# Weights of the gate and up projections placed 64 bytes further on in SBUF, in a cross-attention and FP4 feed-forward kernel

## The chip, the cores and the metric

The kernel runs on one core of a Trainium2 chip. The metric is the device time of one execution in microseconds (us), as the median of several runs. Times inside an execution are read from one profiled run.

## The reference, cut to what matters

The input `x` has 2 x 2048 rows of 512 numbers, and the context has 2 x 77 rows. All is float32. The second layer, on which the change bears, rounds its inputs and weights to a 4-bit grid in blocks of 16:

```python
x = x + xattn(layernorm(x), ctx, ctx)        # 16 heads of 32, causal, 77 keys
def ffn(x):                                  # x 512 wide, hidden 1408 wide
    gate = fp4_linear(x, w_gate)
    y = fp4_linear(x, w_up)
    return fp4_linear(silu(gate) * y, w_down)
x = x + ffn(layernorm(x))
```

## The kernel before, in words

**Tiles and stages.** The 4096 rows are 32 tiles of 128 (`T`). `attention` handles tile after tile: the query projection into `q_ps`, scores, probabilities, values, and the output projection into `w_ps`. Beside it, it rounds the feed-forward weights piece by piece. `feed_forward` then takes the 32 tiles again. In its iteration `a`, TensorE (PE) does `gate(a, c)` and `up(a, c)` for four chunks `c` of 352 hidden columns (`GU_N`), and then `down(a - 2)`, 33 matmuls with 512 columns into `d_ps`. Between chunk 0 and chunk 1 stands one small transposition (L1410). The order on every engine is written out by hand, and tiles 4 to 29 run in a hardware loop.

**Products in three parts.** A product of two float32 matrices is made of a high and a low half of each operand: `split_matmuls` (L177 to L179) issues three matmuls for each of the four slices `d` of 128 input columns, that is 12 for one `gate` or `up` and 12 for one projection:

```python
pe.matmul(out, lh, rh, start=(i == 0), stop=False)      # L177
pe.matmul(out, lh, rl, start=False, stop=False)         # L178
last = pe.matmul(out, ll, rh, start=False, stop=...)    # L179
```

The first operand is stationary: it is loaded into the array before the matmul (LDWEIGHTS, PEld in the profile). The second is moving: it is read from SBUF while the matmul runs. For `gate` and `up` the stationary operand is a slice of `xnh` or `xnl` (`hqh` and `hql` for tile 1 alone, by `halves_of`), and the moving one is 352 columns of `wguh` or `wgul`, 1408 bytes in each partition. These two hold the gate weights in their first 1408 columns and the up weights in the other 1408. For `down` it is `hqh` or `hql` and 512 columns of `wd`, save for the last two tiles, whose halves lie in the space of `wguh` and `wgul` and whose sums go to `u_ps`.

**Places in SBUF.** `sbuf_tensor` gives each tensor the next free place, in the order in which the program asks, rounded up to 32 bytes in a partition. `attention` and `feed_forward` each use the space that lies behind `Shared` and `FfnInput`, one after the other. `wguh` and `wgul` lie over the tensors of `Setup`, which are dead by the time the weights are written there.

From this follow the places below, as the remainder of a tensor's first byte by 256. A slice `d` of `wguh` is 11264 bytes on (44 x 256), the up half is 5632 bytes on (22 x 256), and chunk `c` is `c` x 1408 bytes on (5.5 x 256), so chunks 0 and 2 have the tensor's own remainder and chunks 1 and 3 lie 128 beside it. The slices of all other operands here are whole multiples of 256 apart.

| tensor | role | before | changed |
|---|---|---|---|
| `wguh`, `wgul`, chunks 0 and 2 | moving, 352 | 128 | 192 |
| `wguh`, `wgul`, chunks 1 and 3 | moving, 352 | 0 | 64 |
| `xnh`, `xnl` | stationary | 0 | 0 |
| `hqh`, `hql` | stationary | 192 | 64 |
| `wd` | moving, 512 | 192 | 64 |
| `wqh`, `wql` | moving, 512 | 224 | 96 |
| `woh`, `wol`; `ath`, `atl` | moving, 512; stationary | 224 | 96 |
| `ident` | moving of the transposes | 128 | 192 |
| `att`; `probs`; `q` | stationary of the transposes | 224; 96; 32 | 96; 224; 160 |
| `xin`, `xn` | rows of x | 0 | 192 |

Of the kernel before, what the change touches and what calls it, by code (L numbers as in the profile page):

```python
# [9 lines left out]
F32R = mybir.dt.float32r  # L10
# [6 lines left out]
P = 128  # L17
B, SEQ, E = 2, 2048, 512
# [3 lines left out]
EC = E // P  # L22
# [41 lines left out]
RING = 5  # L64
# [25 lines left out]
class Part:  # L90


    def __init__(self, lo=None, hi=None):
        self.cols = slice(lo, hi)
        self.blocks = slice(lo and lo // BLK, hi and hi // BLK)
# [111 lines left out]
class Shared:  # L207


    def __init__(self, ctx, nc):  # L210
        sb = lambda name, shape, dt=F32: ctx.enter_context(nc.sbuf_tensor(name, shape, dt))
        self.setup = Setup(nc)
        self.wguh, self.wgul = sb("wguh", [P, EC, 2 * FF], F32R), sb("wgul", [P, EC, 2 * FF], F32R)
        self.ident = sb("ident", [P, P])

        self.half_neg, self.eps = sb("half_neg", [P, 1]), sb("eps", [P, 1])
        self.minus_one, self.over_qmax = sb("minus_one", [P, 1]), sb("over_qmax", [P, 1])

        self.xin = sb("xin", [P, RING, E])
        self.xn = sb("xn", [P, E])  # L220
        self.xnh, self.xnl = sb("xnh", [P, EC, P], F32R), sb("xnl", [P, EC, P], F32R)
        self.w_q = sb("w_q", [P, E])
        self.quant = Quant(ctx, nc, "quant", E)

        self.xn_ps = ctx.enter_context(nc.psum_tensor("xn_ps", [P, 512], F32))
        self.x1_stored, self.wd_stored = ctx.enter_context(nc.semaphore("x1_stored")), ctx.enter_context(nc.semaphore("wd_stored"))
# [1561 lines left out]
```

## Time and profile before

| | |
|---|---|
| median of 3 runs | 1170.78 us (1170.64 to 1171.21) |
| the profiled execution | 1172.72 us, its span 1170.9 us |
| TensorE (PE) busy | 1151.4 us, 98% of the span |
| weight loads (PEld) busy | 1042.8 us, 89% |
| VectorE (DVE) busy | 970.1 us, 83% |
| ScalarE (ACT) busy | 482.4 us, 41% |
| GpSimd (POOL) busy | 180.0 us, 15% |
| granted TensorE clock | full through the span |

The span is the time from the first to the last instruction in the profile; the execution's own time holds what lies around it. Matmuls overlap in the profile: a matmul's duration includes the time until its last result is out, and the next one starts before that. What one matmul costs in a dense run is therefore the distance between two starts. The timeline gives starts to 0.01 us, so over 23 distances in a row the mean is known to about 0.5 ns.

### The profile page before, as it was taken

How to read it: one execution, taken by the hardware profiler on the slowest of the kernel's cores; microseconds unless marked ns; L12 is line 12 of the kernel's file. 1: busy time of each engine (PE TensorE's matmuls, PEld its weight loads, DVE VectorE, ACT ScalarE, POOL GpSimd, SP SyncE). 2: the span in 40 equal slices, each digit the busy share in tenths (PEclk: the TensorE clock that was granted, in tenths of full speed). 3: DMA queues.
4: the chain of work that ended last, by engine and by line, in shares of the span. 5: the costliest groups of instructions: out<-in, count | busy, mean ns of one | idle time of the engine just before them, and what ended most of it. 6: DMA issues, size and time to landing. Idle time of an engine off the chain costs nothing.

```text
span 1170.9 us, 21792 instructions
## 1 busy us (share of the span) xinstructions
PE 1151.4 (98%) x6916; PEld 1042.8 (89%) x6916; DVE 970.1 (83%) x1609; ACT 482.4 (41%) x1201; POOL 180.0 (15%) x305
## 2 busy tenths in 40 slices
PE   7899999999999989999999999999999999999998
PEld 6688888888888889999999999999999999999997
DVE  6778888888888877898888888888888888888865
ACT  3556656565666642333322333333333223323321
POOL 2433333333333310100000000000000000000000
PEclk9999999999999999999999999999999999999999
DMA  7133332333445327563454335444533554453352
GB/s 241 35 101 105 92 105 91 104 100 101 141 132 156 120 87 226 118 115 70 94 98 90 88 82 102 81 90 95 96 79 88 99 87 88 87 106 71 84 84 45
DMA packets 139473, 119.26 MB, mean 102 GB/s; under 512 B 91637, under 2 KB 102981, under 8 KB 139180
## 3 DMA queue, kind: packets, MB, share of 16 engines
q1 hardware_dynamic: 139436, 118.83, 43.2%
q8 instruction: 16, 0.26, 0.1%
q14 instruction: 21, 0.17, 0.1%
HBM read 74.47 MB, written 24.94 MB: 85 GB/s over the span
## 4 chain that ended last, share of the span: by engine, by line
PE 91%; DVE 4%; ACT 2%; issue 1%; DMA 1%; POOL 0%; SPq 0%; DVEq 0%; ACTq 0%; POOLq 0%
PE g_ps L177 7%; PE u_ps L177 7%; PE g_ps L178 7%; PE u_ps L178 7%; PE u_ps L179 7%; PE g_ps L179 7%; PE d_ps L1443 6%; PE d_ps L1444 6%; PE d_ps L1442 6%; PE o_ps L792 6%; PE s_ps L730 3%; PE s_ps L772 2%; PE w_ps L177 2%; PE q_ps L178 2%; PE q_ps L179 2%; PE q_ps L177 2%
## 5 line engine op out<-in xcount | busy, mean ns | idle before, releaser
L177 PE MATMUL g_ps<-wguh,xnh 128*128 128x352 f32 x496 | 162.4, 327 | 0.5 <-issue 0.5
L177 PE MATMUL u_ps<-wguh,xnh 128*128 128x352 f32 x496 | 159.9, 322 | 0.4 <-DVE hid L1583 0.4
L178 PE MATMUL u_ps<-wgul,xnh 128*128 128x352 f32 x496 | 159.8, 322 | 0.0
L178 PE MATMUL g_ps<-wgul,xnh 128*128 128x352 f32 x496 | 159.8, 322 | 0.0
L179 PE MATMUL u_ps<-wguh,xnl 128*128 128x352 f32 x496 | 159.6, 322 | 0.0
L179 PE MATMUL g_ps<-wguh,xnl 128*128 128x352 f32 x496 | 159.5, 322 | 0.0
L905 ACT ACTIVATE probs<-s_ps,nsmax 128x77 f32<-128x77 f32 x512 | 114.1, 374 | 88.1 <-DVE nsmax L997 88.1
L1583 DVE TENSOR_TENSOR hid<-u_ps,silu 128x352 f32<-128x352 f32 x128 | 66.9, 523 | 77.7 <-PE u_ps L179 75.5
L1444 PE MATMUL d_ps<-wd,hql 128*128 128x512 f32 x330 | 128.9, 391 | 0.0
L1443 PE MATMUL d_ps<-wd,hqh 128*128 128x512 f32 x330 | 128.9, 391 | 0.0
L1442 PE MATMUL d_ps<-wd,hqh 128*128 128x512 f32 x330 | 128.4, 389 | 0.0
L1485 ACT ACTIVATE silu<-g_ps 128x352 f32<-128x352 f32 x128 | 58.6, 461 | 133.5 <-PE g_ps L179 133.5
L276 POOL TENSOR_TENSOR nmean<-f_mv,minus_one 128x1 f32<-128x1 f32 x32 | 6.1, 192 | 637.7 <-DVE f_mv L271 637.7
L148 ACT ACTIVATE quant_magic<-quant_z 128x512 bf16<-128x512 f32 x65 | 41.1, 633 | 132.1 <-DVE quant_z L142 79.5
L177 PEld LDWEIGHTS g_ps<-wguh,xnh 128*128 128x128 f32 x496 | 93.1, 188 | 2.6 <-issue 0.9
L178 PEld LDWEIGHTS g_ps<-wgul,xnh 128*128 128x128 f32 x496 | 93.3, 188 | 1.1
L177 PEld LDWEIGHTS u_ps<-wguh,xnh 128*128 128x128 f32 x496 | 93.1, 188 | 0.8 <-DVE hid L1583 0.7
L179 PEld LDWEIGHTS u_ps<-wguh,xnl 128*128 128x128 f32 x496 | 93.4, 188 | 0.0
L179 PEld LDWEIGHTS g_ps<-wguh,xnl 128*128 128x128 f32 x496 | 93.4, 188 | 0.0
L178 PEld LDWEIGHTS u_ps<-wgul,xnh 128*128 128x128 f32 x496 | 93.2, 188 | 0.0
L792 PEld LDWEIGHTS o_ps<-vbd,probsT 128*128 128x128 f32 (+1 forms) x640 | 73.9, 191 | 5.1 <-issue 5.0
L792 PE MATMUL o_ps<-vbd,probsT 128*128 128x66 f32 (+2 forms) x640 | 78.2, 277 | 0.0
(177 smaller groups left out, 2524.6 us busy)
## 6 DMA issues: line engine op xcount, KB each, us to landing
scale_wide<-st_dram SPq DMA_DIRECT2D x248, 88.0 KB, 3.4
xin<-in_x_dram SPq DMA_DIRECT2D x32, 256.0 KB, 2.7
x_dram<-x SPq DMA_DIRECT2D x32, 256.0 KB, 2.2
xin<-x_dram SPq DMA_DIRECT2D x32, 256.0 KB, 2.7
out_dram<-y SPq DMA_DIRECT2D x32, 256.0 KB, 2.0
scale_wide<-st_dram SPq DMA_DIRECT2D x248, 32.0 KB, 1.8
w_wide<-ws_dram SPq DMA_DIRECT2D x30, 256.0 KB
wd_dram<-wd_out SPq DMA_DIRECT2D x11, 512.0 KB, 3.5
```

The source lines that it names most:

```text
L148: s.activation(self.magic[:, part.cols], self.z[:, part.cols], ACT.Copy, scale=ULP_SHIFT).then_inc(self.shifted_ready, 1)
L177: pe.matmul(out, lh, rh, start=(i == 0), stop=False)
L178: pe.matmul(out, lh, rl, start=False, stop=False)
L179: last = pe.matmul(out, ll, rh, start=False, stop=(i == n - 1))
L730: last = pe.transpose(s_ps[0:rows, i // 4, (i % 4) * P:(i % 4 + 1) * P], probs[:, at:at + rows], ident[:])
L792: last = pe.matmul(o_ps[:, half, h0 * VW:(h1 + 1) * VW], probsT[0:rows, i, :], vbd[0:rows, b, half, c, 0:(h1 - h0 + 1) * VW], start=(c == ...
L905: last = act.activation(probs[:, h * CTX:(h + 1) * CTX], s_ps[:, bank, i * CTX:(i + 1) * CTX], ACT.Exp, bias=nsmax[:, at:at + 1], scale=1.0)
L1442: pe.matmul(total, high[:, c, :], wd[:, 0, c, :], start=(c == 0), stop=False)
L1443: pe.matmul(total, high[:, c, :], wd[:, 1, c, :], start=False, stop=False)
L1444: summed = pe.matmul(total, low[:, c, :], wd[:, 0, c, :], start=False, stop=(c == FC - 1))
L1485: act.activation(silu[:, c % 2, :], g_ps[:, c % 2, 0:GU_N], ACT.Silu).then_inc(silu_ready, 1)
L1583: dve.tensor_tensor(hid[:, c * GU_N:(c + 1) * GU_N], u_ps[:, c % 2, 0:GU_N], silu[:, c % 2, :], ALU.mult).then_inc(hid_ready, 1)
```

## The change

Sixteen float32 columns (64 bytes in a partition) that nothing uses are asked for ahead of `Setup`, and so ahead of `wguh` and `wgul`. Another 64 unused bytes stand ahead of `xnh`, and the four one-column constants move from ahead of `xin` to behind `xnl`. Together these leave `xnh` and `xnl` at the byte where they were. All that is asked for behind them lies 128 bytes further on, except the constants themselves. No instruction is added, removed or moved on any engine; only addresses differ.

```diff
     def __init__(self, ctx, nc):
         sb = lambda name, shape, dt=F32: ctx.enter_context(nc.sbuf_tensor(name, shape, dt))
+        sb("ahead_of_wguh", [P, 16])
         self.setup = Setup(nc)
         self.wguh, self.wgul = sb("wguh", [P, EC, 2 * FF], F32R), sb("wgul", [P, EC, 2 * FF], F32R)
         self.ident = sb("ident", [P, P])
 
+        self.xin = sb("xin", [P, RING, E])
+        self.xn = sb("xn", [P, E])
+        sb("ahead_of_xnh", [P, 16])
+        self.xnh, self.xnl = sb("xnh", [P, EC, P], F32R), sb("xnl", [P, EC, P], F32R)
         self.half_neg, self.eps = sb("half_neg", [P, 1]), sb("eps", [P, 1])
         self.minus_one, self.over_qmax = sb("minus_one", [P, 1]), sb("over_qmax", [P, 1])
-
-        self.xin = sb("xin", [P, RING, E])
-        self.xn = sb("xn", [P, E])
-        self.xnh, self.xnl = sb("xnh", [P, EC, P], F32R), sb("xnl", [P, EC, P], F32R)
         self.w_q = sb("w_q", [P, E])
```

## Rows read from the trace of the kernel before

**Rows 1.** The page: engines' busy time, and the chain that ended last, by engine.
```profile
PE 1151.4 (98%) x6916; PEld 1042.8 (89%) x6916; DVE 970.1 (83%) x1609; ACT 482.4 (41%) x1201; POOL 180.0 (15%) x305
...
PE 91%; DVE 4%; ACT 2%; issue 1%; DMA 1%; POOL 0%; SPq 0%; DVEq 0%; ACTq 0%; POOLq 0%
```

**Rows 2.** PE's waits: who waited for whom, us in total, times, longest.
```profile
PE tp L651 <- DMA w_nat<-in_L_xattn_Wk_dram: 4.8, 1, 4.8
PE w_ps L721 <- DVE att L1010: 2.6, 1, 2.6
PE tp L651 <- DMA w_nat<-in_L_xattn_Wq_dram: 1.8, 1, 1.8
```

**Rows 3.** Timeline of PE, tile 15: start us, duration us, the instruction.
```profile
760.61 0.32 PE L177 MATMUL g_ps<-wguh,xnh 128*128 128x352 f32 x1
...
764.25 0.32 PE L179 MATMUL u_ps<-wguh,xnl 128*128 128x352 f32 x1
764.41 0.27 PE L1410 MATMUL hq_ps<-ident,scale_cols 128*120 128x128 f32 x1
```

**Rows 4.** The same: chunk 1's second matmul, the first of chunks 2 and 3.
```profile
764.68 0.33 PE L178 MATMUL g_ps<-wgul,xnh 128*128 128x352 f32 x1
...
768.39 0.32 PE L177 MATMUL g_ps<-wguh,xnh 128*128 128x352 f32 x1
...
772.19 0.33 PE L177 MATMUL g_ps<-wguh,xnh 128*128 128x352 f32 x1
```

**Rows 5.** The same: the first matmul of down, and of tile 16.
```profile
776.03 0.39 PE L1442 MATMUL d_ps<-wd,hqh 128*128 128x512 f32 x1
...
783.55 0.32 PE L177 MATMUL g_ps<-wguh,xnh 128*128 128x352 f32 x1
```

**Rows 6.** Timeline of PE, tile 1: bounds of chunks 0, 1, 2 and 3.
```profile
445.01 0.32 PE L178 MATMUL g_ps<-wgul,hqh 128*128 128x352 f32 x1
...
448.53 0.32 PE L179 MATMUL u_ps<-wguh,hql 128*128 128x352 f32 x1
...
449.94 0.32 PE L178 MATMUL g_ps<-wgul,hqh 128*128 128x352 f32 x1
...
453.63 0.32 PE L177 MATMUL g_ps<-wguh,hqh 128*128 128x352 f32 x1
...
457.46 0.32 PE L177 MATMUL g_ps<-wguh,hqh 128*128 128x352 f32 x1
...
461.14 0.32 PE L179 MATMUL u_ps<-wguh,hql 128*128 128x352 f32 x1
```

**Rows 7.** Timeline of PE, attention: the query projection, and the transposes behind it.
```profile
295.36 0.40 PE L178 MATMUL q_ps<-wql,xnh 128*128 128x512 f32 x1
...
297.69 0.39 PE L179 MATMUL q_ps<-wqh,xnl 128*128 128x512 f32 x1
297.92 0.60 PE L721 MATMUL w_ps<-ident,att 128*128 128x128 f32 x4
298.36 1.25 PE L730 MATMUL s_ps<-ident,probs 128*128 128x128 f32 x10
299.45 0.60 PE L698 MATMUL q_ps<-ident,q 128*128 128x128 f32 x4
```

**Rows 8.** Timeline of PE: the output projection, second and twelfth matmul, one iteration.
```profile
300.57 0.40 PE L178 MATMUL w_ps<-wol,ath 128*128 128x512 f32 x1
...
302.88 0.39 PE L179 MATMUL w_ps<-woh,atl 128*128 128x512 f32 x1
```

**Rows 9.** The same, the iteration that was entered after a wait.
```profile
95.89 0.40 PE L178 MATMUL w_ps<-wol,ath 128*128 128x512 f32 x1
...
98.17 0.39 PE L179 MATMUL w_ps<-woh,atl 128*128 128x512 f32 x1
```

**Rows 10.** Timeline of PE, tile 2, chunk 0: second and last matmul.
```profile
461.62 0.32 PE L178 MATMUL g_ps<-wgul,xnh 128*128 128x352 f32 x1
...
465.28 0.33 PE L179 MATMUL u_ps<-wguh,xnl 128*128 128x352 f32 x1
```

## The prediction, made before the changed kernel was run

> **What bounds the kernel now.** I read the page first, then PE's waits, then PE's timeline. The page shows PE busy for 98% of the span and on 91% of the chain that ended last [rows 1]. The reader should then see in the list of waits that PE's longest are single events: 4.8 us for the first weights, 2.6 us and 1.8 us elsewhere [rows 2]. None of them comes back with each tile, so in both stages the next matmul starts as soon as PE can take it. The time is the sum of distances between PE's starts, and a change that moves no instruction can only act by making those distances longer or shorter, or by slowing another engine so far that PE waits.
>
> The distances are the third thing to read, in tile 15, one of 26 that run in the same loop. Chunk 0 has 24 matmuls, 23 distances from 760.61 to 764.25: 3.64 / 23 = **158.3 ns** [rows 3]. Chunk 1 from its second matmul to the start of chunk 2 takes 3.71 us for 23 distances, **161.3 ns**; chunk 2 takes 3.80 us for 24, **158.3 ns** [rows 4]; chunk 3 takes 3.84 us for 24, **160.0 ns** [rows 4, 5]. These four groups do the same work, with the same shapes, at the full clock. What differs between even and odd chunks is the remainder of the moving operand, 128 against 0, while the stationary operand has 0 in both. So the place matters, by about 2 to 3 ns in 160.
>
> **Which relation matters.** The distances depend either on the moving operand's own remainder, or on its difference from the stationary one. Two places speak for the difference. The output projection and the down projection both have a difference of 0, at remainders 224 and 192. The output projection runs at 2.31 / 10 = 231 ns [rows 8], and in the iteration entered after a wait at 2.28 / 10 = 228 ns [rows 9]; the down projection runs at 7.52 / 33 = 227.9 ns [rows 5]. The query projection, equally wide but with a difference of 224, runs at 2.33 / 10 = 233 ns [rows 7]. Equal differences lie closer together than unequal ones, though by little.
>
> **Gate and up, the term of the sum.** After the change the stationary operand stays at 0 and the moving one is at 192 in chunks 0 and 2 and at 64 in chunks 1 and 3. The trace of before already holds these differences once. Tile 1 takes its stationary operand from `hqh` and `hql`, at 192, so its differences are 128 - 192, that is 192 by 256, in the even chunks, and 0 - 192, that is 64, in the odd ones. Its distances are 3.52 / 22 = 160.0 ns in chunk 0, 3.69 / 23 = 160.4 in chunk 1 (whose first few are still settling), 3.83 / 24 = 159.6 in chunk 2 and 3.68 / 23 = 160.0 in chunk 3 [rows 6]. I take **160.0 ns for all four**. Per tile that is now 24 x (158.3 + 161.3 + 158.3 + 160.0) = 15.31 us, and then 96 x 160.0 = 15.36 us: +0.05 us. Over the 30 tiles 2 to 31, **+1.5 us**. The bounds of this term are the other rhythms that 352-column matmuls show. From below, 158.3 ns in all chunks is 15.20 us, -0.11 us a tile, -3.3 us in all. From above stands tile 2's chunk 0, with 3.66 / 22 = 166.4 ns at the usual addresses [rows 10]: a chunk that runs so costs 24 x 6.4 = 0.15 us a tile, +4.6 us over 30 tiles. I take the value of tile 1, because it alone has the differences in question.
>
> **The query projection.** Its difference goes from 224 to 96, and no row has 96. It has 12 matmuls in each of 32 tiles, 384. If the new place gave the 227 to 228 ns of the down projection, it would save 5 to 6 ns each, -2.3 us; the mirror of it, +2.3 us, is my upper bound, since nothing wider than 233 ns stands in the trace at this width. I take 0: 96 and 224 are both an odd multiple of 32, and 233 ns is the only row with such a difference.
>
> **Output and down projections.** All their operands move by 128 together, so the difference stays 0 and I take 0. What may alter is the entry. The output projection settles only after some matmuls, and how it is entered decides between 231 and 228 ns: 0.03 us a tile, -1.0 us at most over 32. The down projection's 7.52 us could fall to 33 x 227 = 7.49, another -0.9 us. An entry worse than the present ones has no row, and I allow the same +1 us. The last two tiles' down matmuls change their difference from 64 to 128, but there are only 66 of them.
>
> **Transposes and everything else.** The `ident` and `xn` places change too. The transposes behind the query projection come at 0.44 / 4 = 110 ns and 1.09 / 10 = 109 ns [rows 7], with three different remainders among their stationary operands and no difference between them: 0. DMA, VectorE, ScalarE and GpSimd work on moved tensors, all still at multiples of 32 bytes. PE waits for none of them in the loops [rows 2], and VectorE has 17% of the span free [rows 1], so a small change there is hidden. If that cover were gone, it would show as a new PE wait in every tile.
>
> **A rule of the Trainium skill against the rows.** What the rows show is that the same matmul takes 158.3 or 161.3 ns by its place [rows 3, 4]. The Trainium skill, "TensorE: Matmul & The Clock Gate", section "Step-by-step: what each phase is for", states that PE has two independent SBUF read ports, and that "Loading the next tile's weights doesn't steal SBUF read bandwidth from the running matmul". By that rule the relation between the two addresses could not matter, and the change would cost 0. This trace does not agree as far as the 2 to 3 ns go, and only for matmuls that read one column per clock; the transposes do agree. The rule keeps a chance below, as a rival.
>
> **The sum.** +1.5 + 0 + 0 = +1.5 us. The profiled execution has 1172.72 us, and its span is 1170.9; the median of the runs is 1170.78, 1.9 lower than the profiled one. The term is the same in both, so the median should go to 1170.78 + 1.5 = **1172.3 us**. About 0.2%, 2.3 us, is what a measurement of this kernel can tell from no change, so this counts as within 0.2%.
>
> **The rivals.**
> - *Faster: a shorter rhythm.* The short rhythm of 158.3 ns appears at difference 128, and tile 1 may be too short a sample to show that the loop falls into it also at 64 and 192. For it: chunk 1 and chunk 3 have the same differences by 256 and still run at 161.3 and 160.0, so the rhythm is not set by the address alone but also by how a chunk is entered. Against it: all four chunks of tile 1 were entered differently and all sit at 160. All chunks at 158.3 give -3.3 us: 1167.5. The query projection at 227 adds to this case, or makes it alone: 1172.3 - 2.3 - 1.0 = 1169.0.
> - *Slower: the long rhythm.* A chunk of the loop is entered in a phase that leads into 166.4 ns and stays there for all its 24 matmuls, as tile 2's chunk 0 does. Since the loop repeats itself exactly, it would happen in every tile or in none. It decides as soon as one chunk of the four is caught: 1172.3 + 4.6 = 1176.9. For it: the rhythm exists at the kernel's own addresses. Against it: 1 of 30 such chunks shows it, and none of tile 1's, and the DMA traffic of that moment may be its cause.
> - *No effect: places do not matter,* and even and odd chunks differ for another reason, such as their position behind the transposition. Chunk 2 and chunk 3 follow each other without a break and still differ, which speaks against it. 1170.8.
>
> **How the numbers follow.** Tile 1's distances hold in the loop: 0.44, of which 0.10 goes over the bound of 1173.1 by the query projection or worse entries. Shorter rhythm, or the query projection and entries together: 0.24. Long rhythm: 0.18. No effect: 0.14. Faster by over 0.2% (below 1168.4): 0.24. Within 0.2%: 0.34 + 0.14 = 0.48. Slower: 0.10 + 0.18 = 0.28. The range goes from 1167.5, the shorter rhythm alone, to 1177.0, one chunk caught in the long one; outside lie deeper savings (0.10) and more than one chunk caught (0.08). The likeliest case's own range is 1169.0 to 1175.6, from -2.3 and -1.0 to +2.3 and +1.0.
>
> **What would show each step.** In the changed kernel's timeline of a loop tile, the distances of chunks 0 to 3 should all be 160 ns; even chunks at 158 mean no dependence on the place, odd ones under 160 the faster rival, any at 166 the slower one. The query projection should keep 233 ns, the transposes 109 to 110, the down projection 227.9 and the output projection 231. PE's waits should be the single ones of before. The forecast is wrong if a chunk's distance is not that of tile 1 of before, or if a new wait of PE comes with each tile.

## The result, and the profile after

| | before | changed |
|---|---|---|
| median, 22 runs each | 1170.66 us | 1172.51 us |
| lowest, highest | 1169.46, 1171.99 | 1171.43, 1174.82 |
| the profiled execution's span | 1170.9 us | 1170.8 us |

The changed kernel is 1.85 us slower, a ratio of 1.0017 with a 95% interval of 1.0011 to 1.0023. The forecast was 1172.3 us, +1.5 us.

The page and PE's waits of the changed kernel, to be read against [rows 1, 2] (columns as there):

```profile
PE 1151.1 (98%) x6916; PEld 1042.5 (89%) x6916; DVE 970.0 (83%) x1609; ACT 481.5 (41%) x1201; POOL 179.8 (15%) x305
```

```profile
PE tp L652 <- DMA w_nat<-in_L_xattn_Wk_dram: 4.7, 1, 4.7
PE w_ps L722 <- DVE att L1011: 2.5, 1, 2.5
PE tp L652 <- DMA w_nat<-in_L_xattn_Wq_dram: 1.8, 1, 1.8
```

The longest waits are those of before; among the shorter ones, single waits of 0.5 us and less differ. No wait comes with each tile. The two spans do not show the difference, because one execution scatters by more than the difference is: from the start of the profile to the first query projection of tile 1 alone, profiles of this study take from 38.9 to 41.2 us. What can be compared between two single profiles is a stretch in which PE never waits. Here is tile 15 of the changed kernel, at the same bounds as in [rows 3 to 5]:

```profile
759.76 0.32 PE L177 MATMUL g_ps<-wguh,xnh 128*128 128x352 f32 x1
...
763.44 0.32 PE L179 MATMUL u_ps<-wguh,xnl 128*128 128x352 f32 x1
...
763.87 0.32 PE L178 MATMUL g_ps<-wgul,xnh 128*128 128x352 f32 x1
...
767.55 0.32 PE L177 MATMUL g_ps<-wguh,xnh 128*128 128x352 f32 x1
...
771.39 0.32 PE L177 MATMUL g_ps<-wguh,xnh 128*128 128x352 f32 x1
...
775.23 0.40 PE L1443 MATMUL d_ps<-wd,hqh 128*128 128x512 f32 x1
...
782.74 0.32 PE L177 MATMUL g_ps<-wguh,xnh 128*128 128x352 f32 x1
```

Chunk 0 takes 3.68 / 23 = 160.0 ns a matmul, chunk 1 (763.87 to 767.55) 3.68 / 23 = 160.0, chunk 2 3.84 / 24 = 160.0, and chunk 3 3.84 / 24 = 160.0. Before they were 158.3, 161.3, 158.3 and 160.0. The down projection takes 7.51 us, where it took 7.52. And tile 1, which had 160 ns in all chunks before [rows 6], now shows this (second and last matmul of chunk 0, first of chunks 2 and 3):

```profile
443.92 0.32 PE L178 MATMUL g_ps<-wgul,hqh 128*128 128x352 f32 x1
...
447.40 0.32 PE L179 MATMUL u_ps<-wguh,hql 128*128 128x352 f32 x1
...
452.48 0.32 PE L177 MATMUL g_ps<-wguh,hqh 128*128 128x352 f32 x1
...
456.28 0.32 PE L177 MATMUL g_ps<-wguh,hqh 128*128 128x352 f32 x1
```

These are 3.48 / 22 = 158.2 ns in chunk 0 and 3.80 / 24 = 158.3 in chunk 2. The weights at 192 meet `hqh` and `hql` at 64, a difference of 128. So tile 1 and the other tiles have changed places with each other, in the kind of their differences (128 and 0 against 192 and 64) and in their rhythm.

### The profile page after: what moved, and what is told of

Its sections match the earlier page's. It is cut to its first block, busy times and chain, and to the rows that moved or that the text cites. A ratio compares the mean times of both kernels' runs of the same rounds, so it can differ in the third digit from the quotient of the medians.

```text
span 1170.8 us, 21792 instructions
## 1 busy us (share of the span) xinstructions
PE 1151.1 (98%) x6916; PEld 1042.5 (89%) x6916; DVE 970.0 (83%) x1609; ACT 481.5 (41%) x1201; POOL 179.8 (15%) x305
## 3 DMA queue, kind: packets, MB, share of 16 engines
q1 hardware_dynamic: 139436, 118.83, 42.7%
## 4 chain that ended last, share of the span: by engine, by line
PE 91%; DVE 4%; ACT 2%; issue 1%; DMA 1%; POOL 0%; SPq 0%; DVEq 0%; ACTq 0%; POOLq 0%
PE g_ps L177 7%; PE u_ps L177 7%; PE u_ps L179 7%; PE u_ps L178 7%; PE g_ps L178 7%; PE g_ps L179 7%; PE d_ps L1445 6%; PE d_ps L1444 6%; PE d_ps L1443 6%; PE o_ps L793 6%; PE s_ps L731 3%; PE s_ps L773 2%; PE q_ps L179 2%; PE q_ps L178 2%; PE w_ps L177 2%; PE q_ps L177 2%
```

## The experiments

The theory is that the **difference**, the first byte of the moving operand less that of the stationary one, as a remainder by 256, sets the distance of the matmuls. The rivals are one operand's own remainder, and a loss that lies in attention. "Rhythm" is the distance, or the repeating pattern of distances, into which a group of matmuls settles. No kernel leaves out any of the computation. Beside each time stands the **tile period** of that kernel's profile: the start of tile 31's first matmul less that of tile 4's, by 27. It is 22.945 us in the profile of before and 22.980 in that of the changed kernel.

**Everything 64 bytes on.** All differences stay, all remainders change; gate and up weights are at 192 and 64, as in the changed kernel.

```diff
+        sb("ahead_of_all", [P, 16])
         self.setup = Setup(nc)
```

> The kernel before with 64 unused bytes ahead of everything, so every operand moves by 64 together: the gate and up weights stand at 192 and 64, as in the changed kernel, but xnh at 64, so each difference is that of before (128 and 0, query 224). Theory (the difference of the two operands sets PE's rhythm): the chunks keep before's 158.3, 161, 158.3 and 160 ns, and the time is that of before, +0 us. Rival (the moving operand's own remainder sets it): all chunks at 160.0 ns, tile period 22.98 us, +1 us or more.

Measured: 1169.71 us against 1170.59, ratio 0.9995 (0.9986 to 1.0004), tile period 22.907 us. Tile 15, at the bounds of chunks 0, 1, 2 and 3:

```profile
759.52 0.32 PE L177 MATMUL g_ps<-wguh,xnh 128*128 128x352 f32 x1
...
763.17 0.32 PE L179 MATMUL u_ps<-wguh,xnl 128*128 128x352 f32 x1
...
763.60 0.33 PE L178 MATMUL g_ps<-wgul,xnh 128*128 128x352 f32 x1
...
767.29 0.32 PE L177 MATMUL g_ps<-wguh,xnh 128*128 128x352 f32 x1
...
771.09 0.32 PE L177 MATMUL g_ps<-wguh,xnh 128*128 128x352 f32 x1
...
774.77 0.32 PE L179 MATMUL u_ps<-wguh,xnl 128*128 128x352 f32 x1
```

The even chunks have 3.65 / 23 = 158.7 and 3.80 / 24 = 158.3 ns, the odd ones 3.69 / 23 = 160.4 and 3.68 / 23 = 160.0. The weights stand where the changed kernel has them, and the rhythm is that of before. The moving operand's own remainder is refuted, and the stationary one's too: it moved here without effect, and in the changed kernel it stayed at 0 while the rhythm changed. Chunk 1 is 1 ns shorter than in the profile of before; more on that below.

**xnh and xnl 64 bytes on.** The gate and up weights keep their places, so the differences are 64 and 192. All that is asked for behind `xnh` moves along by 64, the query, output and down projections' operands together, so their differences stay (save for the last two tiles' down matmuls, which go from 64 to 128).

```diff
+        sb("ahead_of_xnh", [P, 16])
         self.xnh, self.xnl = sb("xnh", [P, EC, P], F32R), sb("xnl", [P, EC, P], F32R)
```

> The kernel before with 64 unused bytes ahead of xnh alone, so the weights stay at 128 and 0 and the stationary operand goes to 64: differences 64 in even and 192 in odd chunks, the query's stays 224. Theory (difference): all chunks at 160.0 ns as in the changed kernel, tile period 22.98 us, query at 233 ns, +1.0 us. Rival (own remainder): nothing moves, tile period 22.95 us.

Measured: 1172.19 us against 1170.59, ratio 1.002 (1.0011 to 1.0029), tile period 22.970 us. Chunk 0 and chunk 2 of tile 15:

```profile
757.51 0.32 PE L177 MATMUL g_ps<-wguh,xnh 128*128 128x352 f32 x1
...
761.19 0.32 PE L179 MATMUL u_ps<-wguh,xnl 128*128 128x352 f32 x1
...
765.30 0.32 PE L177 MATMUL g_ps<-wguh,xnh 128*128 128x352 f32 x1
...
769.14 0.32 PE L177 MATMUL g_ps<-wguh,xnh 128*128 128x352 f32 x1
```

160.0 ns in both. The gate and up weights have not moved, and the changed kernel's rhythm and its longer tile period are there. With the first experiment this settles from both sides that the difference decides. The median of the times is a weaker witness: six of the eleven lie between 1170.2 and 1172.2 us and five between 1173.9 and 1174.5. The upper group lies where a fall of the clock would put it (further on), but no profile shows one of its runs.

**The query projection's share.** From the kernel before, and from the changed kernel, attention's own tensors 128 bytes on; of all the projections' differences this moves the query's alone (before: from 224 to 96; changed: back from 96 to 224). The operands of the transposes, `att`, `probs` and `q`, move against `ident` too.

```diff
         ident = k.ident
+        sb("ahead_of_att", [P, 32])
         ident16 = sb("ident16", [P, P], BF16)
```

> The kernel before with 128 unused bytes at the start of attention's own tensors: only the query projection's difference changes, from 224 to 96; gate and up as before. Theory: the query projection shows two rhythms, 233.2 and 235.1 ns, as in the changed kernel's profile, the iteration stays at 11.96 to 11.99 us, between -0.5 and +0.7 us on the time, and the chunks are those of before. Rival (most of the measured +1.85 us lies in attention): +0.9 us or more.

> The changed kernel with 128 unused bytes at the start of attention's own tensors, so the query's difference is 224 again and only gate, up and the last two down projections differ from before. Theory: +1.2 us (30 tiles of +0.034 us, the last two down projections +0.2 us), iteration of attention 11.973 us. Rival (attention carries the loss): under +0.7 us.

Measured with only the query moved: 1170.17 us, ratio 0.9995 (0.9986 to 1.0004), tile period 22.907. With only gate and up moved: 1172.91 us, ratio 1.0017 (1.0008 to 1.0027), tile period 22.980. The loss stays with gate and up. In the changed kernel's own profile the query projection has two rhythms, shown here by its second and twelfth matmul in two iterations:

```profile
102.08 0.39 PE L178 MATMUL q_ps<-wql,xnh 128*128 128x512 f32 x1
...
104.41 0.40 PE L179 MATMUL q_ps<-wqh,xnl 128*128 128x512 f32 x1
...
282.53 0.41 PE L178 MATMUL q_ps<-wql,xnh 128*128 128x512 f32 x1
...
284.88 0.40 PE L179 MATMUL q_ps<-wqh,xnl 128*128 128x512 f32 x1
```

These are 2.33 / 10 = 233 and 2.35 / 10 = 235 ns. The expectation that the kernel with only the query moved would show both did not hold: in 30 of its 32 iterations it has 233.

**The query at difference 0.** The same place, 32 bytes (`[P, 8]`) in place of 128.

> The kernel before with 32 unused bytes at the start of attention's own tensors, so the query projection's difference goes from 224 to 0; gate and up as before. Theory: the query projection runs at 227 to 231 ns like the output and down projections, which have the same difference, in place of 233: iteration of attention 11.90 to 11.95 us in place of 11.973, -0.7 to -2.3 us. Rival (the query's slower rhythm has another cause): 233 ns and no change.

Measured: 1169.46 us against 1170.96, ratio 0.9988 (0.9979 to 0.9997), tile period 22.947. Two iterations of the query projection:

```profile
101.82 0.40 PE L178 MATMUL q_ps<-wql,xnh 128*128 128x512 f32 x1
...
104.10 0.40 PE L179 MATMUL q_ps<-wqh,xnl 128*128 128x512 f32 x1
...
281.75 0.39 PE L178 MATMUL q_ps<-wql,xnh 128*128 128x512 f32 x1
...
284.06 0.40 PE L179 MATMUL q_ps<-wqh,xnl 128*128 128x512 f32 x1
```

2.28 / 10 = 228 ns, and 2.31 / 10 = 231, in place of 233 [rows 7]. These are the two figures of the output projection [rows 8, 9], whose difference is 0 too. With the difference the query projection took over the other's rhythm. The output projection itself, whose difference did not move, became shorter as well: 229 ns in 18 iterations, where it was 232 in 27 of 32 in before's profile. So part of the gain may be its, by way of how it is entered; the run does not divide the two.

**A difference that is no multiple of 64.** `[P, 8]` ahead of `xnh`: 96 in even chunks, 224 in odd ones.

> The kernel before with 32 unused bytes ahead of xnh, so the gate and up differences are 96 in even and 224 in odd chunks, no multiple of 64; the query's stays 224. Theory (the difference sets the rhythm, and 32 beside a multiple of 64 costs the query projection 233 in place of 227 ns): every chunk at about 166 ns in place of 158 to 161, tile period about 23.6 us, +17 to +20 us. Rival (32 bytes matter only with 512 columns): chunks at 160 ns, +1 us.

Measured: 1176.29 us against 1170.96, ratio 1.0042 (1.0026 to 1.0057), tile period 23.120. Chunks 0, 2 and 3:

```profile
761.80 0.32 PE L177 MATMUL g_ps<-wguh,xnh 128*128 128x352 f32 x1
...
765.55 0.32 PE L179 MATMUL u_ps<-wguh,xnl 128*128 128x352 f32 x1
...
769.67 0.32 PE L177 MATMUL g_ps<-wguh,xnh 128*128 128x352 f32 x1
...
773.56 0.32 PE L177 MATMUL g_ps<-wguh,xnh 128*128 128x352 f32 x1
...
777.24 0.33 PE L179 MATMUL u_ps<-wguh,xnl 128*128 128x352 f32 x1
```

163.0 ns in chunk 0 (3.75 / 23), 162.1 in chunk 2 (3.89 / 24), and 160.0 in chunk 3 (3.68 / 23). The direction was right and the size was not: +5.3 us where 17 to 20 were expected. The difference of 224, dear for the 512 columns of the query projection, costs 352 columns nothing against 64 or 192. What a difference costs does not carry over from one width to another.

**Both kernels once more.**

> The kernel before itself, for the spread of its own executions. Two runs with before's differences showed a tile period of 22.907 us and before's profile 22.945 us, with chunk 1 at 160.0 or 161.1 ns. Theory (the rhythm is caught anew in every execution): this profile shows one of these two, and the two groups of times stand about 30 x 0.038 = 1.1 us apart. Rival: the period is fixed by the addresses, 22.945 us. Time +0 us.

> The changed kernel itself. Theory: tile period 22.98 us in every execution, attention's iteration at 11.94 to 11.99 us, and +1 to +2 us on the time. Those of its times near 1174.7 are executions in which the granted clock falls at the handover from attention to feed-forward, as in the profiles of the two kernels that showed matmuls of 293 ns there; if this profile is one of them, the stretch from 415 to 425 us shows a clock under 1.00. Rival (the high times come from gate and up): a tile period over 23.0 us.

Measured: before 1170.47 us, ratio to its other runs 0.9998 (0.9989 to 1.0007), tile period **22.907**; changed 1172.65 us, ratio 1.0015 (1.0006 to 1.0024), tile period 22.980. In this profile of before, chunk 1 of tile 15 runs from 762.02 to 765.71, and the down projection from 773.35 to 780.85:

```profile
762.02 0.33 PE L178 MATMUL g_ps<-wgul,xnh 128*128 128x352 f32 x1
...
765.71 0.32 PE L177 MATMUL g_ps<-wguh,xnh 128*128 128x352 f32 x1
...
773.35 0.39 PE L1442 MATMUL d_ps<-wd,hqh 128*128 128x512 f32 x1
...
780.85 0.32 PE L177 MATMUL g_ps<-wguh,xnh 128*128 128x352 f32 x1
```

Chunk 1 has 3.69 / 23 = 160.4 ns, where the first profile of the same program had 161.3 [rows 4], and the down projection 7.50 us, where it had 7.52 [rows 5]. These are the two halves of the 0.04 us by which a tile is shorter. The kernel before has two states of its loop, 22.907 and 22.945 us a tile, and each profile stays in one from tile 6 to tile 31. Six profiles were taken of kernels with before's gate and up differences: four show 22.907 and two (before itself, and the query at 0) 22.945 or 22.947. The three profiles with the changed differences and `xnh` at 0 all show 22.980. Two groups of times 1.1 us apart, as expected, cannot be told apart in the eleven times of this run.

The profile of the kernel with only gate and up moved (1175.31 us) shows something else, in the windows from 230 to 415, from 415 to 425 us and behind (PE, weight loads, VectorE, ScalarE, GpSimd busy us and counts; then the granted clock, DMA share, GB/s), and in the timeline of PE:

```profile
230.00:415.00 185.00, 184.64 (x1257) 157.98 (x1256) 158.81 (x336) 113.79 (x377) 62.82 (x76) 1.00 0.41 126
415.00:425.00 10.00, 7.44 (x34) 7.06 (x33) 7.94 (x19) 7.35 (x24) 1.07 (x4) 0.66 0.17 49
425.00:1171.00 746.00, 743.87 (x4208) 698.25 (x4206) 613.47 (x861) 226.77 (x380) 33.54 (x120) 1.00 0.46 94
```

```profile
417.92 1.12 PE L723 MATMUL w_ps<-ident,att 128*128 128x128 f32 x4 [2.56 <-DVE att L1012]
418.83 2.34 PE L732 MATMUL s_ps<-ident,probs 128*128 128x128 f32 x10
...
421.26 0.49 PE L178 MATMUL g_ps<-wgul,xnh 128*128 128x352 f32 x1
421.55 0.49 PE L179 MATMUL g_ps<-wguh,xnl 128*128 128x352 f32 x1
421.85 0.49 PE L177 MATMUL g_ps<-wguh,xnh 128*128 128x352 f32 x1
```

The matmuls come at 290 to 300 ns, 352 columns at 1.2 GHz, the lower of the clock's two levels. PE had waited 2.56 us for VectorE just before. That wait is in every profile (2.1 to 2.6 us), before's too [rows 2], but the clock was 1.00 throughout this window in before's profile and in the changed kernel's first. The profile with only the query moved has 0.66 there as well, though its gate and up differences are those of before, so the fall does not belong to them. The second profile of the changed kernel, a run of 1173.00 us, has a shorter fall:

```profile
415.00:425.00 10.00, 8.34 (x41) 7.52 (x42) 7.15 (x18) 6.11 (x18) 1.08 (x4) 0.83 0.15 57
```

The profiles with the query at 0 and with `xnh` 32 bytes on have 0.83 there too. From the query projection of attention's tile 31 to tile 1 of feed-forward the two profiles at 0.66 take 44.0 and 43.7 us, the changed kernel's second 42.7, and the first profiles of before and changed, without a fall, 42.0 and 41.7. So a fall costs up to 2 us. This fits a group of 5 of the changed kernel's 22 times, between 1174.3 and 1174.8.

**Differences 0 and 128 swapped.** `[P, 32]` ahead of `xnh`.

> The kernel before with 128 unused bytes ahead of xnh: the weights stay at 128 and 0, xnh and xnl go to 128, so the differences change places: 0 in even chunks and 128 in odd ones; the query's stays 224. Theory (difference): chunks 0 and 2 at 160 to 161 ns, chunks 1 and 3 at 158.3 ns, tile period 22.90 to 22.95 us, time -1 to +1 us. Rival (even chunks are the short ones for their own place or their turn in the order): chunks 0 and 2 stay at 158.3.

Measured: 1169.99 us against 1170.56, ratio 1.0002 (0.9991 to 1.0013), tile period 22.917. Chunks 0, 2 and 3:

```profile
757.48 0.32 PE L177 MATMUL g_ps<-wguh,xnh 128*128 128x352 f32 x1
...
761.16 0.32 PE L179 MATMUL u_ps<-wguh,xnl 128*128 128x352 f32 x1
...
765.23 0.32 PE L177 MATMUL g_ps<-wguh,xnh 128*128 128x352 f32 x1
...
769.07 0.32 PE L177 MATMUL g_ps<-wguh,xnh 128*128 128x352 f32 x1
...
772.71 0.33 PE L179 MATMUL u_ps<-wguh,xnl 128*128 128x352 f32 x1
```

Now chunk 3 is the short one, 3.64 / 23 = 158.3 ns, and chunks 0 and 2 have 160.0. The short rhythm followed the difference of 128 to the other chunks.

**A version that beats both.** Everything 64 bytes on, and the query at difference 0 (both edits from above).

> The kernel before with 64 unused bytes ahead of everything and 32 more at the start of attention's own tensors: gate and up have before's differences at other places, the query projection's difference is 0. Theory: the sum of the two single changes, tile period 22.91 or 22.95 us, query projection at 227 to 231 ns, -1 to -2 us. Rival (the gain of the query at difference 0 was an accident of that kernel's places): query at 233 ns, +0 us.

Measured: **1168.35 us** against 1170.56, ratio 0.9984 (0.9975 to 0.9992), tile period 22.907, query projection 228 and 231 ns. That is 2.2 us under the kernel before, and it repeats the gain of the single change at other places. Between this kernel and the one with only the query at 0, the intervals do not decide.

## Why the prediction was right

**The bound.** PE bounds the kernel and no instruction moved, so only distances count: confirmed, the waits are the same and the tiles' distances carry the difference.

**Gate and up, +1.5 us.** The 160.0 ns for all four chunks was read from tile 1 and came out in every chunk of the loop tile above, so the faster rival, 158.3 ns also at 64 and 192, did not occur. The 96 matmuls of the four chunks now take 96 x 160.0 ns = 15.36 us, as forecast. Against the profile that the prediction had, the whole tile gained 22.980 - 22.945 = 0.035 us, not 0.05, so 1.0 us over 30 tiles; the distances inside chunks explain 0.05, the down projection gave back 0.01 (7.51 for 7.52), and the rest lies where chunks and stages are entered. Against the other state of before it is 22.980 - 22.907 = 0.073 us, 2.2 us over 30 tiles. The measured +1.85 lies between. The term was right in its mechanism. That its size came so near is in part luck: the profile at hand showed the slower of two states of which the prediction did not know, and the sum had no term for the clock at the handover.

**Difference, not remainder.** The prediction had it from distances at 512 columns that differ "by little", 228 and 231 ns against 233. The whole shift by 64, the shift from `xnh` on by 64, and the swap by 128 now show it three times, and tile 1 of the changed kernel a fourth time.

**The query projection, 0.** Its new difference gave 233 or 235 ns for 233, and the kernel with it alone has no measurable change. Taking 0 was right as a number. The reason given for it, that 96 and 224 are both an odd multiple of 32, does not hold in general: at 352 columns the two differ, 162 to 163 ns against 160.0. This part was luck. The bound below, 227 to 228 ns at -2.3 us, is what difference 0 gives in half of the iterations.

**Output and down projections, 0.** Nearly so: the down projection takes 7.51 for 7.52 us, and attention from its first query matmul to that of tile 31 takes 381.9 us for 382.0. One thing was passed over too lightly: the last two tiles' down matmuls went from 64 to 128. The first row pair bounds the last 41 of these 66 matmuls before, the second the same ones in the changed kernel:

```profile
1158.15 0.40 PE L1443 MATMUL u_ps<-wd,wguh 128*128 128x512 f32 x1
...
1167.32 0.40 PE L1444 MATMUL u_ps<-wd,wgul 128*128 128x512 f32 x1
```

```profile
1157.88 0.39 PE L1444 MATMUL u_ps<-wd,wguh 128*128 128x512 f32 x1
...
1167.22 0.40 PE L1445 MATMUL u_ps<-wd,wgul 128*128 128x512 f32 x1
```

9.17 / 40 = 229 ns became 9.34 / 40 = 233.5, which over 66 matmuls is +0.3 us. At 512 columns the difference of 128 is a poor one, at 352 the best.

**The rival of the long rhythm** did not occur. In tile 2's chunk 0 the first profile of before alone has 166 ns [rows 10]; the eleven others, the second profile of the same program among them, have 158 to 162 there. One more profile, that of the swap, has the long rhythm for ten distances in chunk 1 of tile 2, and none has it in a loop tile. So the addresses alone do not decide it. What leads into it stays open.

**The rule that weights load without taking read bandwidth from the running matmul** ("TensorE: Matmul & The Clock Gate", section "Step-by-step: what each phase is for", in the Trainium skill) gave 1170.8 us. For these matmuls the runs decide against the consequence that the prediction drew from it: the same work takes 158.3 to 163.0 ns as the difference of the two addresses is changed. Whether the two reads are what meets there was not measured.

**What stays open.** Why a difference acts as it does was not measured; the runs show that it does, not the circuit. Nor does the difference fix the rhythm alone: at 0, chunk 1 and chunk 3 differ within one tile, and chunk 1 between two executions. Six of the twelve profiles show a fall of the clock at the handover, one of the changed kernel's two and neither of before's two. How often the clock falls at the handover in each kernel, and how much of the +1.85 us that is, would take many more profiles. It is not all of it: without the five times of 1174.3 us and more the changed kernel's median is still 1172.10 us, 1.44 above before's, and the two lowest times, 1171.43 and 1169.46, are 1.97 apart.

## What to carry to other kernels

Where PE never waits, look at the distance between its starts group by group, for equal work that runs at unequal pace, and compare the first bytes of moving and stationary operand by 256. For a cheap fix, shift one tensor by 32 to 128 bytes, and judge it by the distances in a profile, since 1 to 2 us in 1170 take some twenty runs to see in the time. Try the difference for each width of its own: in this kernel 128 was best for 352 columns, and 0 for 512.

## What was not expected of the hardware

- One program has two loop states that last for hundreds of microseconds: 22.907 and 22.945 us a tile, in different executions. In one, chunk 1's matmuls come at 160.4 ns and down takes 7.50 us, in the other at 161.3 ns and 7.52 us.
- The settled rhythms depend on width and difference together. 352 columns: 158.3 ns at 128; 160.0 (or 161) at 0; 160.0 at 64, 192 and 224; 162 to 163 at 96. 512 columns: 227 to 232 ns at 0 (it takes some matmuls to settle); 229 at 64; 232 to 233 at 224; 233 or 235 at 96; 232 to 233.5 at 128.
- After one and the same wait of 2.5 to 2.6 us, the granted clock fell to 1.2 GHz for some microseconds in some profiles and not in others, the same program's among them.
